# A graph attention block: normalised tokens turned by a transposing transfer in place of TensorE

## The reference

```python
h = jnp.maximum(_layernorm(x, axis=-1), 0.0)
q, k, v = (split_heads(h @ W.T) for W in (Wq, Wk, Wv))       # 16 heads of 32
a = einsum('bhnd,bhmd->bhnm', q, k) * 512**-0.5 + 2 * adj     # adj is both encodings
a = where(any(a != 0, axis=-1), a, -inf)
p = softmax(a, axis=-1)                                       # NaN becomes 0
x = x + (p @ v, heads joined) @ Wo.T
```

## Time and profile before

| | |
|---|---|
| median of 3 runs | 1256.42 us (1256.36 to 1258.66) |
| profiled execution | 1256.68 us, span 1254.9 us |
| TensorE busy | 1228.8 us, 98% |
| VectorE busy | 1068.1 us, 85% |
| ScalarE busy | 1044.8 us, 83% |
| GpSimd busy | 898.7 us, 72% |
| one batch in the loop | 38.09 us |

### The profile page before, as it was taken

One profiled execution on the slowest core, in us unless ns is written; L12 is line 12 of the kernel. 1 busy time (PEld: TensorE's weight loads), 2 busy tenths in 40 slices (PEclk: granted clock), 3 DMA queues, 4 the chain that ended last, 5 costly groups with the idle time before them and its releaser, 6 DMA issues.

```text
span 1254.9 us, 43727 instructions
## 1 busy us (share of the span) xinstructions
PE 1228.8 (98%) x13104; PEld 1108.5 (88%) x13104; DVE 1068.1 (85%) x3500; ACT 1044.8 (83%) x2427; POOL 898.7 (72%) x1266
## 2 busy tenths in 40 slices
PE   6899999999999999999999999999999999999997
PEld 5788989989989989889889899899999899898996
DVE  6788888888888888888888888888888888888887
ACT  5888888888888888888888888888888888888886
POOL 4767777777776777777777776777767777767765
PEclk9999999999999999999999999999999999999999
DMA  7355445465445464454564454654454554545533
GB/s 241 90 125 151 117 111 141 116 159 137 122 109 138 130 150 132 121 124 124 144 150 117 112 141 116 158 139 120 109 138 129 150 133 118 126 125 142 134 98 88
DMA packets 90773, 163.89 MB, mean 131 GB/s; under 512 B 14976, under 2 KB 23168, under 8 KB 90752
## 3 DMA queue, kind: packets, MB, share of 16 engines
q1 hardware_dynamic: 90752, 163.64, 50.3%
HBM read 46.14 MB, written 16.78 MB: 50 GB/s over the span
## 4 chain that ended last, share of the span: by engine, by line
PE 83%; issue 5%; DVE 5%; POOL 4%; ACT 3%; DMA 0%; DVEq 0%; ACTq 0%; POOLq 0%
PE job_ps L330 48%; PE pT_ps L405 15%; PE s_ps L394 8%; PE o_ps L426 5%; PE job_ps L345 2%; PE o_ps L427 2%; POOL fold L1006 2%; PE job_ps L370 2%; DVE minus L801 1%; ACT pT_hi L627 1%; DVE stats L694 1%; DVE pT_lo L810 1%; ACT probs L616 1%; ACT y L597 1%; POOL bounds L1012 0%
## 5 line engine op out<-in xcount | busy, mean ns | idle before, releaser
L1006 POOL TENSOR_TENSOR fold<-minus 128x512 f32<-128x512 f32 x256 | 326.7, 1276 | 245.2 <-DVE bounds L801 245.0
L616 ACT ACTIVATE probs<-minus,bounds 128x256 f32<-128x256 f32 x1024 | 461.6, 503 | 9.2 <-DVE bounds L801 9.1
L810 DVE TENSOR_TENSOR pT_lo<-pT_ps,pT_hi 128x512 f16<-128x512 f32 x512 | 350.7, 685 | 122.6 <-ACT pT_hi L627 122.2
L801 DVE CUSTOM_DVE_ANT_0 minus<-s_ps,adj_now 128x256 f32<-128x256 f32 x1024 | 389.3, 418 | 12.7 <-issue 6.1
L627 ACT ACTIVATE pT_hi<-pT_ps 128x512 f16<-128x512 f32 x512 | 305.9, 597 | 107.9 <-PE pT_ps L405 106.3
L405 PE MATMUL pT_ps<-ident,probs 128*128 128x128 f32 x2048 | 307.5, 273 | 1.7 <-ACT probs L616 1.6
L330 PE MATMUL job_ps<-hT_hi,w_hi 128*128 128x256 f16 x1024 | 280.2, 274 | 1.6 <-DVE hT_lo L762 1.2
L330 PE MATMUL job_ps<-hT_hi,w_lo 128*128 128x256 f16 x1024 | 278.9, 272 | 0.0
L330 PE MATMUL job_ps<-hT_lo,w_hi 128*128 128x256 f16 x1024 | 278.8, 272 | 0.0
L405 PEld LDWEIGHTS pT_ps<-ident,probs 128*128 128x128 f32 x2048 | 241.9, 140 | 19.0 <-ACT probs L616 2.3
L394 PE MATMUL s_ps<-qk_stack 96*128 96x256 f32 x1024 | 246.7, 323 | 2.1 <-DVE w_lo L748 1.2
(11 more groups left out here) (88 smaller groups left out, 2190.4 us busy)
## 6 DMA issues: line engine op xcount, KB each, us to landing
qk_stack<-qk_parts SPq DMA_DIRECT2D x768, 128.0 KB, 2.3
x_in<-x SPq DMA_DIRECT2D x32, 512.0 KB, 4.9
x_res<-x SPq DMA_DIRECT2D x32, 512.0 KB, 3.8
out<-y SPq DMA_DIRECT2D x64, 256.0 KB, 2.1
adj_in<-adj SPq DMA_DIRECT2D x32, 256.0 KB, 4.8
w_in<-wq SPq DMA_DIRECT2D x2, 512.0 KB, 6.0
w_in<-wk SPq DMA_DIRECT2D x2, 512.0 KB, 7.6
w_in<-wv SPq DMA_DIRECT2D x2, 512.0 KB, 9.6
```

Of the source, the lines that this page charges most:

```text
L616: end = nc.scalar.activation(probs[hh % 2][:, t, :], minus[hh // 2 % 2][:, hh % 2, t, :], ACT.Exp, bias=bounds[:, hh // 2 % 4, 2 * (hh % 2 ...
L801: end = nc.vector.tensor_tensor_reduce(out=minus[pair % 2][:, hh % 2, t, :], in0=s_ps[SCORE_BANK[hh]][:, t * N:(t + 1) * N], in1=adj_now[: ...
L810: nc.vector.tensor_tensor(pT_lo[hh % 4][:, :, :], pT_ps[hh % 2][:, :].rearrange("p (m n) -> p m n", m=NT), pT_hi[hh % 4][:, :, :], ALU.sub ...
L1006: nc.gpsimd.tensor_tensor(f1[:, :, :], src[:, :, 0:N // 2], src[:, :, N // 2:N], ALU.add).then_inc(folded1, 1)
```

## The change

From batch 1 on the tokens are split before they are turned. In slot 9 ScalarE writes max(h, 0) in f16 for the whole batch (split_tokens) into h_parts, and VectorE writes the remainder of one token tile each in slots 11 and 15 (low_tokens). h_parts holds for each of the two token tiles 1024 f16 columns: 512 high, 512 low. ScalarE then issues a transposing transfer for each tile (turn_tokens), for tile 0 in slot 13 of batch b and for tile 1 in slot 1 of batch b + 1, into hT, which now has two buffers that alternate from batch to batch. Both follow the copy of the probabilities in their slot. The h jobs are gone from JOBS, so TensorE turns only the tokens of batch 0. The products read the new layout: for q and k the moving operand is two runs of 128 columns.

The statistics move to slots 3 and 6, normalise to slot 7. The loops of TensorE and ScalarE have two batches in their bodies. In batch 0 the jobs stand in another order (q and k job 2 ahead of v 0), the first weight splits are signalled by halves, the first stack of q and k goes in two parts, v 0 has a bank of its own, Wo is split in four pieces in slots 6 to 13, and the tokens of batch 1 are split and turned in slots 0 to 3.

```diff
@@ -27,8 +27,8 @@
     3: [("v", 3, 0, 3, 12), ("o", 1, -1, 0, 4)],
-    4: [("h", 0, 1, 0, 4), ("y", 0, -1, 0, 6)],
-    5: [("y", 0, -1, 6, 9), ("h", 1, 1, 0, 4), ("y", 0, -1, 9, 12)],
+    4: [("y", 0, -1, 0, 6)],
+    5: [("y", 0, -1, 6, 12)],
     6: [("qk", 0, 1, 0, 12)],
@@ -45,6 +45,8 @@
+OTHER_BANK = [("v", 1, 0), ("qk", 3, 0), ("v", 2, 0), ("v", 3, 0)]
 PER_BATCH = {"h": 2, "qk": 4, "v": 4, "o": 2, "y": 2}
@@ -118,8 +120,8 @@
         y = sb("y", [P, NT, D])
-        hT_hi = sb("hT_hi", [P, KT, N], F16)
-        hT_lo = sb("hT_lo", [P, KT, N], F16)
+        h_parts = sb("h_parts", [P, NT, 2, D], F16)
+        hT = [sb(f"hT{i}", [P, NT, 2 * KT, P], F16) for i in range(2)]
...
@@ -251,6 +264,16 @@
+            def first_stack(n):
+                sp.wait_ge(taken["qk"], count("qk", n, 0))
+                for j in range(G):
+                    for r, pair in enumerate((slice(1, 3), slice(0, 3, 2), slice(1, 4, 2))):
+                        sp.dma_start(qk_stack[HD * r:HD * (r + 1), 0, j, :, n, :].bitcast(F32),
+                                     qk_parts[HD * j:HD * (j + 1), 0, pair, n, :].bitcast(F32)
+                                     ).then_inc((stacked, late_stacked)[n][j], 16)
             def load_tokens(b):
@@ -264,14 +287,14 @@
             sp.dma_start(adj_in[:, :, :], adj_d[0]).then_inc(adj_loaded, 16)
+            load_tokens(1)
             for half in range(2):
             sp.dma_start(x_res[:, :, :], x_d[0]).then_inc(res_loaded, 16)
-            load_tokens(1)
-            stack(0, 0, True)
+            for n in range(2):
+                first_stack(n)
             def body(b, first, last):
@@ -330,36 +353,43 @@
-            hT = (hT_hi, hT_lo)
             oT = (oT_hi, oT_lo)
-            def job(kind, n, d, start, stop, b):
+            def job(kind, n, d, start, stop, b, odd=0):
+                tokens = hT[(odd + d) % 2]
                 ps = job_ps[bank(kind, n, b + d)]
-                        pe.wait_ge(h_ready, b + (d + 1))
+                        pe.wait_ge(h_ready, 1)
                     for k, t in [divmod(i, NT) for i in range(start, stop)]:
-                        end = nc.tensor.transpose(ps[:, k * N + t * P:k * N + (t + 1) * P],
+                        end = nc.tensor.transpose(ps[:, t * N + k * P:t * N + (k + 1) * P],
                                                   h[:, t, (2 * n + k) * P:(2 * n + k + 1) * P], ident[:, :])
                     half = PRODUCTS["qk"] // 2
+                    early = isinstance(b, int) and b + d == 0
                     if n == 0 and start == 0:
-                        pe.wait_ge(taken["h"], count("h", 0, b + d))
-                    if n == 0 and start <= half // 2 < stop:
-                        pe.wait_ge(taken["h"], count("h", 1, b + d))
+                        if early:
+                            pe.wait_ge(taken["h"], 1)
+                        else:
+                            for turned in h_turned:
+                                pe.wait_ge(turned, (b + d) * 16)
+                    if early and n == 0 and start <= half // 2 < stop:
+                        pe.wait_ge(taken["h"], 2)
                     for i, w in enumerate((WQ, WK)):
                         if start < (i + 1) * half and stop > i * half:
-                            end = product(ps[:, i * N:(i + 1) * N],
+                            end = product(ps[:, i * N:(i + 1) * N].rearrange("p (t n) -> p t n", t=NT),
                                           [lambda k, w=m: w[:, k, n * P:(n + 1) * P] for m in (w_hi[w], w_lo[w])],
-                                          [lambda k, v=v: v[:, k, :] for v in hT], start - i * half, stop - i * half)
+                                          [lambda k, a=a: tokens[:, :, a * KT + k, :] for a in range(2)],
+                                          start - i * half, stop - i * half)
                 elif kind == "v":
                     t, half = n % NT, n // NT
-                    end = product(ps[:, 0:HALF], [lambda k, v=v: v[:, k, t * P:(t + 1) * P] for v in hT],
+                    end = product(ps[:, 0:HALF], [lambda k, a=a: tokens[:, t, a * KT + k, :] for a in range(2)],
                                   [lambda k, w=w: w[:, k, half * HALF:(half + 1) * HALF] for w in (w_hi[WV], w_lo[WV])],
@@ -383,7 +413,10 @@
             def scores(b, hh, early=False):
-                if hh % HH < G:
+                if isinstance(b, int) and b == 0 and G <= hh < HH:
+                    pe.wait_ge(late_stacked[hh % G], STACKED)
+                elif hh % HH < G:
...
@@ -450,25 +490,27 @@
             turn(WK, 0)
-            weight_waits(pe, WQ, 0)
-            job("qk", 0, 0, 0, 12, 0)
-            weight_waits(pe, WK, 0)
-            job("qk", 0, 0, 12, 24, 0)
+            for i in range(4):
+                pe.wait_ge(first_split, i + 1)
+                job("qk", 0, 0, 6 * i, 6 * (i + 1), 0)
             job("qk", 1, 0, 0, 24, 0)
             turn(WV, 1)
+            weight_waits(pe, WQ, 1)
+            job("qk", 2, 0, 0, 12, 0)
+            weight_waits(pe, WK, 1)
+            scores(0, 0, True)
+            job("qk", 2, 0, 12, 24, 0)
+            scores(0, 1, True)
             weight_waits(pe, WV, 0)
-            scores(0, 0, True)
             job("v", 0, 0, 0, 12, 0)
-            scores(0, 1, True)
-            job("qk", 2, 0, 0, 24, 0)
-            job("v", 1, 0, 0, 12, 0)
             weight_waits(pe, WV, 1)
             scores(0, 2, True)
-            def body(b, first, last):
+            job("v", 1, 0, 0, 12, 0)
+            def body(b, odd, first, last):
                 for hh in range(HEADS):
@@ -482,16 +524,17 @@
                     for kind, n, d, start, stop in jobs_at(hh, first, last):
-                        job(kind, n, d, start, stop, b)
+                        job(kind, n, d, start, stop, b, odd)
                 for i, (kind, n, d) in last_in.items():
-            body(0, True, False)
-            pe.wait_ge(wo_split, 2)
-            with pe.Fori(1, B - 1) as b:
-                body(b, False, False)
-            body(B - 1, False, True)
+            body(0, 0, True, False)
+            pe.wait_ge(wo_split, KT)
+            with pe.Fori(1, B - 1, 2) as b:
+                body(b, 1, False, False)
+                body(b + 1, 0, False, False)
+            body(B - 1, 1, False, True)
             def last_turn(k):
...
@@ -627,6 +673,26 @@
+            def turn_tokens(b, t, odd, first):
+                act.wait_ge(h_split, (b - 1) * NT + (t + 1))
+                settled(act, "act")
+                if not first:
+                    act.wait_ge(ended["qk"], count("qk", 0, b - 1))
+                    settled(act, "act")
+                act.dma_start_transpose(hT[odd][:, t, :, :], h_parts[:, t, :, :].rearrange("p a d -> p (a d)")
+                                       ).then_inc(h_turned[t], 16)
+            def split_tokens(b, first):
+                act.wait_ge(h_ready, b + 1)
+                if not first:
+                    for turned in h_turned:
+                        act.wait_ge(turned, (b - 1) * 16)
+                nc.scalar.activation(h_parts[:, :, 0, :], h[:, :, :], ACT.Relu).then_inc(h_high, 1)
             def copy_adj(b):
@@ -641,20 +707,22 @@
             sum_weight(WQ, 1)
-            sum_weight(WV, 0)
             act.wait_ge(q_scales, 1)
             take("qk", 0, 0, True)
+            sum_weight(WV, 0)
             sum_weight(WV, 1)
             take("qk", 1, 0, True)
-            for i, half in TURNS[2:]:
-                high_weight(i, half)
+            high_weight(WQ, 1)
+            high_weight(WK, 1)
+            high_weight(WV, 0)
             copy_adj(0)
+            high_weight(WV, 1)
             exponentials(0, 0, True)
-            take("v", 0, 0, True)
             act.wait_ge(q_scales, 2)
             take("qk", 2, 0, True)
-            def body(b, first, last):
+            take("v", 0, 0, True)
+            def body(b, odd, first, nearly, last):
                 for hh in range(HEADS):
@@ -668,17 +736,32 @@
                         take(kind, n, b + d, first and (kind, d) in (("v", 0), ("qk", 0)))
-                    if first and hh in (3, 5):
-                        high_out_weight(hh // 2 - 1)
-                    if hh == HEADS - 3 and not last:
+                    if first and 6 <= hh < 6 + KT:
+                        high_out_weight(hh - 6)
+                    if hh == HEADS - 3 and not (first or last):
                         copy_adj(b + 1)
                     high_probs(b, hh, first and hh < 4)
-            body(0, True, False)
-            with act.Fori(1, B - 1) as b:
-                body(b, False, False)
-            body(B - 1, False, True)
+                    if hh == HEADS - 3 and first:
+                        copy_adj(b + 1)
+                    if first and hh == 0:
+                        split_tokens(1, True)
+                    if not (nearly or last) and hh == 9:
+                        split_tokens(b + 2, False)
```

(57 more changed lines are left out.)

71 lines of the change are left out of this document (48 added, 23 removed).

## The result

The changed kernel takes 1390.71 us, median of 4 runs (1387.65 to 1395.48); the kernel before, beside it on the same chip, 1256.78. The ratio is 1.1067, 95% interval 1.105 to 1.1084. I had forecast 1228, with 1221 to 1264 as the range. The profiled execution took 1387.65 us with a span of 1385.9.

What follows compares the result with a forecast made beforehand. TensorE, busy 98% of the span, was taken to bound the kernel. 1256.7 - 27.9 (TensorE) + 1.5 (holds) - 2.5 (batch 0) = 1227.8, so 1228 us; its own range 1221 to 1234, with rivals 1221 to 1264.

Steps and rivals of the forecast that it cites:

- TensorE, -27.9: Slots 4 and 5: removing the fp32 token transposes saves 0.90 us in each of 31 batches, split operands costing nothing.
- The holds, +1.5: Slots 13 and 1: ScalarE's two transposing-transfer issues stay hidden; 1.5 us in all added in case X reaches 1.0.
- X: Time one transposing transfer's issue holds ScalarE's queue; taken as 0.65 us, bounded between 0.37 and 3.0.
- the cover: Slack hiding X: up to 0.95 us in slot 13, resting on a shift 0.6 us earlier, and 1.3 in slot 1.
- rival 1: ScalarE's queue eats part of the gain, X between 1.0 and 1.65; at X = 1.4, 1243 us; chance 0.22.
- "Nothing" for ScalarE's split in slot 9: The 1.058 us Relu replaces two 0.592 us copies; waits for TensorE in odd slots absorb it, so no cost.
- "Nothing" for VectorE's low parts: Slots 11 and 15: low parts from SBUF priced like those from PSUM, 0.6 to 0.7 us, no cost in sum.
- Batch 0, -2.5: Reordered first batch wins back some 3 us of waits against added work; between +4 and -5, taken as -2.5 us.
- The transfers' data, +0: Each 256 KB transposing transfer takes 1.3 us of the DMA engines and lands in time, costing nothing.
- rival 3: Transposing transfers' data late at 4 us each, delaying slot 2's stack pieces to head 8's scores: 18 us, 1243; chance 0.07.
- the mean misleads: Caution that the mean slack a batch, 5.8 us on ScalarE and 5.2 on VectorE, is not a safe guide.
- the highest figure of any rival: Rival of ScalarE's queue eating more than the whole gain: 1280 us at X = 2.0, some 1340 at 3.0; chance 0.18.

Runs made afterwards that it cites:

- deep: copied with tokens one batch further ahead, statistics and normalise in slots 7, 11, 12, split tile by tile in slots 5 and 6, low parts behind: 1231.56 us.
- rework: Kernel before with only batch 0's new order and the new token layout; fp32 transposes stay, no split or transposing transfers: 1255.04 us.
- holds: Kernel before plus two transposing transfers of unused buffers a batch, issued by ScalarE in slots 13 and 1: 1290.35 us.
- deep_act: deep with the transposing transfers issued by ScalarE in slots 13 and 1, still into hT_next, one batch per body: 1268.58 us.
- copied: Changed kernel with SyncE issuing the transposing transfers into hT_next, a plain copy of each tile to one hT, and one-batch loop bodies: 1277.36 us.
- loop2_pe: Kernel before with TensorE's loop body holding two batches, ScalarE's one: 1289.4 us.
- deep_loop2: deep with TensorE's loop body holding two batches, ScalarE's one: 1271.41 us.
- copied_later: copied with the split moved from slot 9 to 10 and the first low part from slot 11 to 12: 1237.05 us.
- later_split: Changed kernel with the split moved from slot 9 to 10 and the first low part from slot 11 to 12: 1321.86 us.
- loop2_act: Kernel before with ScalarE's loop body holding two batches, TensorE's one: 1276.06 us.

## Why the prediction was wrong, point by point

**TensorE, -27.9: right, and visible once the rest is mended.** In deep TensorE is busy 1201.3 us for 1228.8, so 27.5 less, and a batch is 0.91 us shorter, where I had 0.90. Split operands are free (rework). In the changed kernel the gain of slot 4 is mostly not there: y 0 waits 0.30 us at 510.87 for VectorE, which now has the first half of the statistics in slot 3. In deep, with these in slot 7, slot 4 takes 2.61 us, for 3.14 before and 3.02 to 3.09 in the changed kernel; that the statistics are the cause is argued, not shown, since deep moves more than them.

**The holds, +1.5: wrong, by the size of X and by the cover.** The place and the chain were right: with adj_now at 489.25 in the earlier trace rows's terms, its end at 489.88, X = 1.45, and the exponentials' 0.8 give 492.1 for the copy of y, and it starts at 492.31. But I took X = 0.65, after the qk_stack pieces; it is 1.26 to 1.58 us but for four longer ones, so on its own numbers rival 1 was the case. Nor was the cover 0.95 and 1.3: in holds it is some 0.65 and 1.0. It rested on the shift of head 15 coming 0.6 us earlier, and ScalarE's wait of 1.10 us before adj_now shrinking with it; that wait is 1.16 us in the changed kernel, and adj_now comes 0.92 us later against TensorE, not 0.6 earlier. The holds cost 1.12 to 1.18 us a batch (holds, deep_act): 35 us, not 1.5, and by themselves more than the transposes give.

**"Nothing" for ScalarE's split in slot 9: wrong.** I priced the instruction (1.06 us, right) and set it against ScalarE's waits, but didn't ask when its input is ready. Normalise, which I let "fit" into slot 7, starts at 478.39 in the batch shown, behind a fold and its statistics' arithmetic; it keeps ScalarE waiting for 1.07 us, with the copies of q and k of slot 9 queued behind. From there VectorE is 2.16 us late. In copied this one instruction costs 0.86 us a batch.

**"Nothing" for VectorE's low parts: wrong.** 0.67 us was the row of a low part from PSUM. From SBUF it takes 0.68 alone and 1.35 beside GpSimd's fold, 1.09 on the mean of 62. Of copied's 1.45 us it costs 0.31 alone, and 0.28 more together with the split. It stands for 1.3 us of statistics in slot 11, so the shifts of slots 12 and 13 come no earlier at all. This is the step on which the cover for the holds stood.

**Two-batch loop bodies: never priced.** The diff shows them in two lines. They cost 1.1 us a batch on the mean in the kernel before (loop2_pe) and 1.44 in deep_loop2; over the whole runs that is 29 and 40 us.

**Batch 0, -2.5: near by itself, not shown for the changed kernel.** rework gives 1.9 us, without the split, the low parts and the two transfers that the change puts in slots 0 to 3. Its profiled execution, a slower one of its ten, reaches the second adj_now 2.9 us earlier than before (63.29 for 66.20) and the third 1.1 later: TensorE waits 2.83 us for wo_lo, at 71.06, which my sum did not name, and the clock falls behind it. The changed kernel's third adj_now starts at 105.35 us, for 103.94 before.

**The transfers' data, +0: near.** TensorE's waits for qk_stack come to 7.4 us over the changed kernel's whole run, 4.1 of them before 110 us, for 0.8 in the kernel before. The 1.3 us was misread: 0.64 us is what the issue of a qk_stack piece takes, not its data. The piece lands after 2.3 us, a transposing transfer after 4.7, near rival 3's 4 us, but from 100 to 1150 TensorE waits for a stack only 4 times, 2.6 us in all. Rival 3's own sum, 1256.7 - 27.9 + 18 - 2.5, gives 1244, not 1243.

**The sum.** Per batch: 38.08 - 0.91 (deep) + 0.22 (copied_later against deep: this order of the work) + 1.45 (copied against copied_later: the slots of the split and its low part) + 1.18 (deep_act) + 1.44 (deep_loop2) = 41.46 us. Measured is 42.66, the mean of both kinds. The 1.2 us left are of the size of the clock's part: the mean granted clock of the span is 0.973, so 0.027 x 1385.9 = 37 us of full speed were lost, 1.2 us in each of 31 batches, against 4 us over the whole run in copied (0.997) and 6 in deep_loop2 (0.995). Each of the costs alone brings stalls that mostly leave the clock alone; together they bring longer ones, and behind some of these TensorE runs at 1.2 GHz for 3 to 4 us. In later_split the mean clock is 0.983, 22 us: so 15 of the 69 us that it gives back are the clock's, and the other 54, 1.7 us a batch, are near the 1.45 of copied. The windows of slots 14, 15 and 0 in batches 3 to 27 show the place: there the lowered clock takes 1.9 us of full speed from a batch that ends in an edge and 0.5 from the others, 1.2 on the mean, in deep_loop2 0.1, in copied and deep_act nothing. A part of it falls on idle time and costs nothing, so 1.2 is the most it can be. What ScalarE's own edge (1.15 us in loop2_act) adds beside it no run separates.

**The failed steps.** Two terms of the sum failed. The holds stood at +1.5 us and cost 1.12 to 1.18 us a batch, some 35 us, as X was 1.3 to 1.5 and not 0.65 and its cover thinner than I had it. And ScalarE's split and VectorE's low parts stood at "nothing" and cost 1.45 us a batch (copied against copied_later), the split because it was set against ScalarE's mean slack and not against the moment at which its input is ready, the low part because its price was that of one from PSUM. A third cost, the two-batch bodies, 1.1 to 1.44 us a batch, stood in no term. I had written that "the mean misleads" and then hid each new cost behind the same slack. Rival 1, X at 1.4, had the right hold and still gave 1243; the highest figure of any rival was 1340.

## What to carry to other kernels

Price a moved instruction at the moment its input is ready, and write down what stands behind it in its queue: moving a copy one slot on, past a wait of 1.1 us for its input, gave back 0.86 us a batch. When several new costs are each hidden by one slack, add them up before you take it. Count the instructions of a loop body: doubling a long one to alternate two buffers cost more here than the 0.91 us that the change could win, and a plain copy of the tile through a second buffer (deep) cost nothing that can be seen.
